# First layer norm of a gated attention and FFN block: rows scaled on ScalarE, `bn_aggr` for the moments, two buffers for the first values, output weights of the second head fetched three quads sooner

## The chip, the cores and the metric

One Trainium2 chip, one of its cores. The metric is the device time of one execution in microseconds (us), the median of several.

## What is computed

A block of a Flamingo model in fp32: 32 x 64 = 2048 rows `x` of 512, the same number of context rows, 32 query heads on 8 key/value heads of 128, causal within each batch entry, then a gated FFN of width 1792 whose weights are each multiplied by a product of rank 4.

```python
x = x + tanh(g_xattn[0]) * xattn(_layernorm(x), ctx, ctx, Wq, Wk, Wv, Wd)
x = x + tanh(g_ffn[0])  * ffn(_layernorm(x), ...)

def _layernorm(x, axis=-1, eps=1e-05):
    m = jnp.mean(x, axis=axis, keepdims=True)
    v = jnp.var(x, axis=axis, keepdims=True)
    return (x - m) / jnp.sqrt(v + eps)
```

## The kernel before, in words

Every fp32 product is made of three fp32r matmuls (`three_pass`, L503): each operand is split in a high part (a copy, on ScalarE) and a low part (the raw value less the high part, on VectorE or POOL). Each engine has its program written out by hand, with semaphores; the order in it is the order of the code, and an engine that waits holds all that stands behind.

The program has four parts. First the keys of half of the context (`keys`, to about 54 us). Then 44 **quads** q = 0 to 43 (to about 526 us), each a product of two by two blocks in Strassen's form with seven products of six matmuls each (`quad` and `product`, L558 to L610): quads 0 to 7 (NV = 8) make the values, 8 to 11 (NK = 4) the other keys, and from Q0 = 12 on the queries, 16 quads for each of two blocks of x. Then 64 attention units with the output product (L694), and the FFN.

A quad on TensorE runs the products 1, 6, 5, then (in some quads) the transposes of x, then 4, 2, 7, the one matmul of `effective` (L551, all quads but 7 and 8), and 3. ScalarE (L883) makes the high part of the next quad's weights (`left_hi`, L858), copies bank 0 to s1 (L894), splits two small factors `el`, `er` (`lr_hi`), copies bank 2 to s5 (L902), and writes a quarter of the result (L918). VectorE (L1167) makes t1 and t2 (L1173, L1185), the low halves of `el` and `er` (L1158), and three quarters of the result (L1196 to L1201); then `effective` (L1165). POOL (L1557) makes the low parts of the next weights (`left_lo`, L1470) and the sums for the quad after (`left_sums`, L1458 to L1463), in quads 0 to 5 the same for the context (`c_sums`, `c_combinations_lo`). SP issues all DMAs in one order (`quad_dmas`, L414): the last result's store, the store and load of `effective`, loads of context, weights, `el` and `er`, and x.

Between these the first layer norm is laid out in steps, for eight pairs of row tiles m = 0 to 7, four for each block of x:

```python
STATS = {q: m for m, q in enumerate((0, 3, 5, 7, 10, 13, 16, 19))}
APPLY, COLUMNS, X_SPLIT = ({q + n: m for q, m in STATS.items()} for n in range(1, 4))
```

In a STATS quad VectorE ends with `bn_stats` on `x_st` (L1122). In the APPLY quad it computes mean and variance + eps from them in seven small instructions (`ln_moments`, L1124 to L1135), POOL raises that to -1/2 (`ln_pow`, L1429), and VectorE ends the quad with (x - mean) * rstd in place (`apply1`, L1143). In the COLUMNS quad TensorE transposes the rows behind its third product (`columns`, L535), ScalarE copies them out (L840, L843), POOL sums them (`x_sums`). In the X_SPLIT quad they are split on ScalarE (L856) and at the end on VectorE (`x_lo`, L1152). The second layer norm uses the same `ln_moments` and `ln_pow` for n = 8 to 15, and POOL applies it (`apply2`).

The values leave from one buffer `v_st` (L357), so VectorE and ScalarE wait in quads 1 to 8 for the last store. The output weights of head k + 1 are fetched to one buffer `wd_raw` at every fourth unit (L474), the first of these in front of unit 2, and split on ScalarE (L928) and POOL (L1476) in the units of WD_STEP.

## Time and profile before

| | |
|---|---|
| median of 3 runs | 1510.31 us (1509.82 to 1510.69) |
| the profiled execution: time, span | 1507.59 us, 1505.6 us |
| mean granted TensorE clock | 0.998 |
| TensorE busy | 1475.6 us (98%) |
| VectorE, ScalarE, POOL busy | 1113.6 (74%), 638.5 (42%), 827.1 us (55%) |

The span goes from the first to the last instruction. A row of the timeline gives start and length in us, engine, line, operation, tile written and tiles read, shapes, the count of like instructions in a row, and in brackets how long the engine had been idle before it and what ended that. PE is TensorE, DVE VectorE, ACT ScalarE, POOL GpSimd, SPq the queue of SP. Matmuls overlap, so that one starts every 0.23 us and takes 0.39.

### The profile page before, as it was taken

The page shows a single profiled execution, that of the slowest core. Times are in us where ns is not written, and L with a number is a line of the kernel's source. Part 1 is how long each engine was busy: PE and PEld are TensorE (multiplying, and loading weights), DVE is VectorE, ACT ScalarE, POOL GpSimd, SP SyncE. Part 2 cuts the span into 40 slices and gives each one's busy share as a digit, 9 for nine tenths or more (in the row PEclk, how much of TensorE's full clock was granted, in tenths as well). Part 3 has the DMA queues.
Part 4 walks back from the last instruction along what each step waited for, and adds up shares of the span by engine and source line. Part 5 has one row for each costly group of instructions (what it writes and reads, how often), then busy time and mean ns, then how long its engine had stood idle before and what let it go on. Part 6 is the DMA issues. An engine that isn't in the chain of part 4 may idle for free.

```text
span 1505.6 us, 20729 instructions
## 1 busy us (share of the span) xinstructions
PE 1475.6 (98%) x7322; PEld 1176.3 (78%) x7322; DVE 1113.6 (74%) x1653; ACT 638.5 (42%) x1099; POOL 827.1 (55%) x716
## 2 busy tenths in 40 slices
PE   8999998999999999999999999999999999999998
PEld 8877777788888777777777777777788888888886
DVE  5387788876667767777777788778588897767676
ACT  5444444444444434344333444444344344434342
POOL 5598988887789311211211332234387877666663
PEclk9999999999999999999999999999999999999999
DMA  7466666767988553333333333342011111311112
GB/s 267 157 223 206 223 216 234 237 232 269 356 270 286 187 186 122 113 131 116 115 140 131 113 131 115 112 146 89 18 46 57 50 56 49 111 51 56 50 56 70
DMA packets 116070, 218.02 MB, mean 145 GB/s; under 512 B 9472, under 2 KB 47616, under 8 KB 113920
## 3 DMA queue, kind: packets, MB, share of 16 engines
q1 hardware_dynamic: 115968, 216.70, 42.7%
q8 instruction: 59, 0.97, 0.3%
q14 instruction: 43, 0.35, 0.1%
HBM read 151.13 MB, written 65.54 MB: 144 GB/s over the span
## 4 chain that ended last, share of the span: by engine, by line
PE 87%; DVE 8%; issue 2%; POOL 1%; DMA 1%; ACT 0%; SPq 0%; DVEq 0%; POOLq 0%; ACTq 0%
PE bank L507 63%; PE bank L659 4%; PE bank L621 4%; PE bank L772 3%; PE bank L774 3%; PE bank L773 3%; PE bank L630 2%; PE bank L644 2%; DVE x_st L1146 1%; DVE t L1185 1%; DVE el L1158 1%; DVE X L1322 1%; DVE xc L1152 1%; DVE er L1158 0%; PE bank L683 0%
## 5 line engine op out<-in xcount | busy, mean ns | idle before, releaser
L1476 POOL TENSOR_TENSOR wd_lo<-wd_raw,wd_hi 128x512 fp32r<-128x512 f32 x64 | 91.4, 1448 | 368.8 <-ACT wd_hi L928 368.8
L507 PE MATMUL bank<-xc,wa_hi 128*128 128x512 f32 x896 | 278.9, 392 | 1.1 <-DVE q_st L1201 0.8
L507 PE MATMUL bank<-wd_hi,o_hi 128*128 128x512 f32 x512 | 205.7, 402 | 0.0
L507 PE MATMUL bank<-wd_hi,o_lo 128*128 128x512 f32 x512 | 200.1, 391 | 0.0
L507 PE MATMUL bank<-wd_lo,o_hi 128*128 128x512 f32 x512 | 199.3, 389 | 0.0
L507 PEld LDWEIGHTS bank<-xc,wa_hi 128*128 128x128 f32 x896 | 167.9, 189 | 39.1 <-DVE q_st L1201 2.1
L507 PE MATMUL bank<-xc,wa_lo 128*128 128x512 f32 x448 | 175.0, 391 | 0.0
L1322 DVE SCALAR_TENSOR_TENSOR X<-bank,tg,X 128x512 f32<-128x512 f32 x224 | 156.4, 741 | 0.0
L507 PE MATMUL bank<-x_hi,wf_hi 128*128 128x512 f32 x392 | 153.0, 390 | 0.2 <-DVE d_lo L1310 0.2
L507 PE MATMUL bank<-x_hi,wf_lo 128*128 128x512 f32 x392 | 152.6, 389 | 0.0
L507 PE MATMUL bank<-x_lo,wf_hi 128*128 128x512 f32 x364 | 141.6, 389 | 0.0
L1217 DVE TENSOR_TENSOR prob<-bank,mask 128x512 f32<-128x512 f32 x64 | 44.3, 692 | 127.5 <-PE bank L630 125.8
L1470 POOL TENSOR_TENSOR wa_lo<-w_raw,wa_hi 128x512 fp32r<-128x512 f32 x72 | 83.2, 1176 | 55.1 <-ACT wa_hi L869 55.1
L507 PEld LDWEIGHTS bank<-wd_hi,o_lo 128*128 128x128 f32 x512 | 96.1, 188 | 20.8
L507 PEld LDWEIGHTS bank<-wd_lo,o_hi 128*128 128x128 f32 x512 | 96.4, 188 | 18.1
L507 PEld LDWEIGHTS bank<-wd_hi,o_hi 128*128 128x128 f32 x512 | 96.2, 188 | 17.9 <-DVE X L1255 0.3
L947 ACT ACTIVATE pt<-bank 128x512 f32<-128x512 f32 x64 | 38.2, 598 | 156.7 <-PE bank L644 156.7
L507 PEld LDWEIGHTS bank<-xc,wa_lo 128*128 128x128 f32 x448 | 84.4, 188 | 18.0
L1255 DVE SCALAR_TENSOR_TENSOR X<-bank,tg,X 128x512 f32<-128x512 f32 x128 | 90.6, 743 | 10.4 <-PE bank L507 10.4
L1517 POOL TENSOR_TENSOR wf_lo<-f_raw,wf_hi 128x512 fp32r<-128x512 f32 (+1 forms) x56 | 57.7, 1032 | 63.1 <-ACT wf_hi L988 62.8
L772 PE MATMUL bank<-dn_hi,d_hi 128*128 128x512 f32 x224 | 87.3, 390 | 0.9 <-DVE X L1322 0.9
L1014 ACT ACTIVATE d_hi<-bank 128x512 fp32r<-128x512 f32 x56 | 33.6, 600 | 128.9 <-DVE bank L1316 68.8
(179 smaller groups left out, 3504.3 us busy)
## 6 DMA issues: line engine op xcount, KB each, us to landing
q_scratch<-q_st SPq DMA_DIRECT2D x32, 1024.0 KB, 4.3
q_sb<-q_scratch SPq DMA_DIRECT2D x64, 512.0 KB, 3.3
w_raw<-in_wq SPq DMA_DIRECT2D x32, 512.0 KB, 4.3
wd_raw<-in_wd SPq DMA_DIRECT2D x16, 1024.0 KB, 4.9
f_raw<-ffn_eff_scratch SPq DMA_DIRECT2D x28, 512.0 KB, 3.6
er_raw<-in_sf_r SPq DMA_DIRECT2D x42, 256.0 KB, 3.6
e_raw<-in_wf SPq DMA_DIRECT2D x42, 256.0 KB, 5.2
ffn_eff_scratch<-e_eff SPq DMA_DIRECT2D x42, 256.0 KB, 5.0
```

The lines of the kernel that those rows point to most:

```text
L507: last = pe.matmul(to, a, b, start=(start and n == 0), stop=(stop and n == 3 * len(pairs) - 1), skip_group_check=onto)
L621: last = pe.matmul(bank[6][b * S:(b + 1) * S, t * 256:(t + 1) * 256], k_sb[u % 2][:, cb * S:(cb + 1) * S], q_sb[u % 2][:, :, cb, :, :].rea ...
L659: last = pe.matmul(bank[4 + b][:, t * 256:(t + 1) * 256], v_sb[u % 2][rows, t, :], pt[rows, t, :], start=True, stop=True)
L772: pe.matmul(to, d_hi[b][:, half, cols], dn_hi[n == NF - 1][:, :], start=True, stop=False)
L773: pe.matmul(to, d_hi[b][:, half, cols], dn_lo[n == NF - 1][:, :], start=False, stop=False)
L774: pe.matmul(to, d_lo[b][:, half, cols], dn_hi[n == NF - 1][:, :], start=False, stop=True).then_inc(p_yf, 1)
L1217: v.tensor_tensor(prob[:, :, :], bank[6][:, :].rearrange("p (n k) -> p n k", k=S), mask[:, :].rearrange("p (o k) -> p o k", o=1).broadcast ...
L1255: v.scalar_tensor_tensor(to, bank[t if u < NU - 1 else 4 + t][:, :], tg[:, 0:1], to, ALU.mult, ALU.add).then_inc(v_y, 1)
L1322: v.scalar_tensor_tensor(to, bank[4 + k % 4][:, :], tg[:, 1:2], to, ALU.mult, ALU.add).then_inc(v_yf, 1)
L1470: g.tensor_tensor(wa_lo[p][:, part, :, :].rearrange("p n k d -> p (n k d)"), raw, f32(wa_hi[p][:, part, :, :]).rearrange("p n k d -> p (n ...
L1476: g.tensor_tensor(wd_lo[h % 2][:, e, :], wd_raw[:, e, :], f32(wd_hi[h % 2][:, e, :]), ALU.subtract).then_inc(g_wd, 1)
L1517: g.tensor_tensor(wf_lo[:, cols, :, :].rearrange("p n k d -> p (n k d)"), raw, f32(wf_hi[:, cols, :, :]).rearrange("p n k d -> p (n k d)") ...
```

## The change

`bn_aggr` gives mean and variance from the six numbers of `bn_stats`, one instruction for each of two row tiles. VectorE then makes variance + eps and the negated mean, POOL the power and `shift` = -mean * rstd, and ScalarE computes x * rstd + shift in place, at the end of its APPLY quad. The last four row pairs are laid out four quads apart and not three. The values of quads 1 and 3 go to a second buffer, whose place is that of the first query weights, so that their load waits for the stores. `load_wd(1)` moves from the first unit to quad 41. Numbers of lines are those before.

```diff
-    STATS = {q: m for m, q in enumerate((0, 3, 5, 7, 10, 13, 16, 19))}
+    STATS = {q: m for m, q in enumerate((0, 3, 5, 7, 11, 15, 19, 23))}
...
+    V_BUFFER = (0, 1, 0, 1, 0, 0, 0, 0)
+    def v_stored(q):
+        return V_BUFFER[:q].count(V_BUFFER[q])
...
     def load_w(w):
             if w < 2:
                 sp.wait_ge(v_wvl, 7)
+                sp.wait_ge(d_vo[1], 16 * 2)
...
         for q in range(NQ):
             quad_dmas(q)
+            if q == NQ - 3:
+                load_wd(1)
...
-            if i % 4 == 0 and i // 4 + 1 < NWD:
+            if i % 4 == 0 and 0 < i and i // 4 + 1 < NWD:
                 load_wd(i // 4 + 1)
...
         def columns(m):
-                pe.wait_ge(v_xn, 2 * m + p + 1)
+                pe.wait_ge(a_xn, 2 * m + p + 1)
...
+        def apply1(m):
+            a.wait_ge(g_nm, m + 1)
+            for p in range(2):
+                a.activation(x_st[:, p, :], x_st[:, p, :], ACT.Identity, bias=shift[:, p:p + 1],
+                             scale=rstd[:, p:p + 1]).then_inc(a_xn, 1)
...
-            if 1 <= q <= NV:
-                a.wait_ge(d_vo, 16 * q)
+            if 2 <= q < NV:
+                a.wait_ge(d_vo[V_BUFFER[q]], 16 * v_stored(q))
...
             a.activation(result(q, 0, 0), split(q, bank[0][:, :]), ACT.Copy).then_inc(a_c11, 1)
+            if q in APPLY:
+                apply1(APPLY[q])
...
         def ln_moments(n):
             v.wait_ge(v_bn, 2 * n + 2)
-            v.tensor_tensor(mean[:, :], bn[:, :, 1], bn[:, :, 4], ALU.add).then_inc(v_ln, 1)
-            v.tensor_tensor(half_gap[:, :], bn[:, :, 1], bn[:, :, 4], ALU.subtract).then_inc(v_ln, 1)
-            v.tensor_tensor(veps[:, :], bn[:, :, 2], bn[:, :, 5], ALU.add).then_inc(v_ln, 1)
-            v.wait_ge(v_ln, 6 * n + 3)
-            v.tensor_scalar(mean[:, :], mean[:, :], 0.5, None, ALU.mult).then_inc(v_ln, 1)
-            v.scalar_tensor_tensor(half_gap[:, :], half_gap[:, :], 0.25, half_gap[:, :], ALU.mult,
-                                   ALU.mult).then_inc(v_ln, 1)
-            v.tensor_scalar(veps[:, :], veps[:, :], 1.0 / D, EPS, ALU.mult, ALU.add).then_inc(v_ln, 1)
-            v.wait_ge(v_ln, 6 * n + 6)
-            v.tensor_tensor(veps[:, :], veps[:, :], half_gap[:, :], ALU.add).then_inc(v_eps, 1)
+            if 1 <= n <= 8:
+                v.wait_ge(g_nm, n)
+            for p in range(2):
+                v.bn_aggr(moments[:, p, :], bn[:, p, :]).then_inc(v_ln, 1)
+            v.wait_ge(v_ln, 2 * n + 2)
+            v.tensor_scalar(veps[:, :], moments[:, :, 1], EPS, None, ALU.add).then_inc(v_eps, 1)
+            if n < 8:
+                v.tensor_scalar(neg_mean[:, :], moments[:, :, 0], -1.0, None, ALU.mult).then_inc(v_nm, 1)
...
-        def apply1(m):
-            v.wait_ge(g_pow, m + 1)
-            for p in range(2):
-                v.tensor_scalar(x_st[:, p, :], x_st[:, p, :], mean[:, p:p + 1], rstd[:, p:p + 1], ALU.subtract,
-                                ALU.mult).then_inc(v_xn, 1)
...
         def ln_pow(n):
             g.wait_ge(v_eps, n + 1)
+            if 1 <= n <= 8:
+                g.wait_ge(a_xn, 2 * n)
             g.tensor_tensor(rstd[:, :], veps[:, :], neg_half[:, :], ALU.pow).then_inc(g_pow, 1)
+            if n < 8:
+                g.wait_ge(g_pow, n + 1)
+                g.wait_ge(v_nm, n + 1)
+                g.tensor_tensor(shift[:, :], neg_mean[:, :], rstd[:, :], ALU.mult).then_inc(g_nm, 1)
```

How it moves instructions, at three places. VectorE from the moments of an apply quad to the next quad, in the kernel before (quad 11; mean, half_gap and veps are the small tiles):

```order
L1126 TENSOR_TENSOR mean<-bn 128x2
L1127 TENSOR_TENSOR half_gap<-bn 128x2
L1128 TENSOR_TENSOR veps<-bn 128x2
L1130 TENSOR_SCALAR mean<-mean 128x2
L1131 SCALAR_TENSOR_TENSOR half_gap<-half_gap 128x2
L1133 TENSOR_SCALAR veps<-veps 128x2
L1135 TENSOR_TENSOR veps<-veps,half_gap 128x2
L1185 TENSOR_TENSOR t_104<-bank,s_101 128x512
...
L1165 TENSOR_TENSOR e_eff<-bank,e_raw_110 128x512
L1146 TENSOR_SCALAR x_st<-x_st,mean,rstd 128x512 x2
L1173 TENSOR_TENSOR t_103<-bank,s_101 128x512
```

and of the change (quad 12):

```order
L1152 BN_AGGR moments<-bn 128x2 x2
L1154 TENSOR_SCALAR veps<-moments 128x2
L1156 TENSOR_SCALAR neg_mean<-moments 128x2
L1198 TENSOR_TENSOR t_106<-bank,s_103 128x512
...
L1178 TENSOR_TENSOR e_eff<-bank,e_raw_112 128x512
L1186 TENSOR_TENSOR t_105<-bank,s_103 128x512
```

Seven small instructions have become four, and the two on `x_st` are gone from between two quads.

ScalarE from the end of the apply quad (the quarter of the result) to the copy of bank 0 to s1, before:

```order
L918 ACTIVATE kq_98<-bank 128x4x128
L869 ACTIVATE wa_hi_93<-w_raw_87 128x512
L871 ACTIVATE wa_hi_93<-w_raw_87 128x256
L874 ACTIVATE wa_hi_93<-ws_91 128x1024
L894 ACTIVATE s_101<-bank 128x512
```

and of the change:

```order
L939 ACTIVATE q_st_101<-bank 128x4x2x64
L852 ACTIVATE x_st<-x_st,shift,rstd 128x512 x2
L888 ACTIVATE wa_hi_93<-w_raw_87 128x512
L890 ACTIVATE wa_hi_93<-w_raw_87 128x256
L893 ACTIVATE wa_hi_93<-ws_91 128x1024
L913 ACTIVATE s_103<-bank 128x512
```

The two activations on `x_st`, with their wait for `shift`, stand ahead of the next weights' high part.

SP at quad 41 of the change:

```order
L347 DMA el_raw_110<-in_sf_l 128x128
L348 DMA er_raw_108<-in_sf_r 128x512
L383 DMA wd_raw<-in_wd 128x2048
L377 DMA q_scratch<-q_st_102 128x4x512
L359 DMA ffn_eff_scratch<-e_eff 128x512
```

and, of the kernel before, where that load stood, behind the last quad:

```order
L367 DMA q_scratch<-q_st_100 128x4x512
L349 DMA ffn_eff_scratch<-e_eff 128x512
L373 DMA wd_raw<-in_wd 128x2048
L382 DMA q_sb_114<-q_scratch 128x1024
L384 DMA k_sb_122<-k_scratch 128x256
```

The load of the second head's output weights has gone ahead of the stores of the queries of quads 41, 42 and 43 and of four loads for the first units.

## Rows read from the trace of the kernel before

**Rows 1.** The page, section 1: busy us, share of the span, instructions.
```profile
PE 1475.6 (98%) x7322; PEld 1176.3 (78%) x7322; DVE 1113.6 (74%) x1653; ACT 638.5 (42%) x1099; POOL 827.1 (55%) x716
```
**Rows 2.** Waits of TensorE: us in total, times, longest.
```profile
PE bank L541 <- DVE x_st L1146: 11.4, 12, 2.0
...
PE bank L507 <- ACT v_st L918: 1.9, 1, 1.9
```
**Rows 3.** Timeline of TensorE: starts behind a wait, quads 5, 7, 9, 12.
```profile
110.81 0.50 PE L507 MATMUL bank<-wv_hi,cc 128*128 128x512 f32 x1 [0.31 <-DVE t L1185]
...
136.72 0.66 PE L541 MATMUL bank<-ident,x_st 128*128 128x128 f32 x4 [1.79 <-DVE x_st L1146]
...
159.31 0.66 PE L541 MATMUL bank<-ident,x_st 128*128 128x128 f32 x4 [1.98 <-DVE x_st L1146]
...
194.44 0.65 PE L541 MATMUL bank<-ident,x_st 128*128 128x128 f32 x4 [1.59 <-DVE x_st L1146]
```
**Rows 4.** Timeline of TensorE: transposes of quad 2; L551 of quads 11, 12, 13.
```profile
80.76 1.12 PE L541 MATMUL bank<-ident,x_st 128*128 128x128 f32 x8
81.64 0.47 PE L507 MATMUL bank<-wv_hi,cc 128*128 128x512 f32 x1
...
186.25 0.50 PE L551 MATMUL bank<-er,el 96*128 96x512 f32 x1
...
199.91 0.40 PE L551 MATMUL bank<-er,el 96*128 96x512 f32 x1
...
209.68 0.40 PE L551 MATMUL bank<-er,el 96*128 96x512 f32 x1
```
**Rows 5.** Timeline of VectorE: moments of quad 4; moments and rows of quad 11.
```profile
107.22 2.24 DVE L1126 TENSOR_TENSOR mean<-bn 128x2 f32<-128x2 f32 x1
...
186.22 0.58 DVE L1126 TENSOR_TENSOR mean<-bn 128x2 f32<-128x2 f32 x1
...
188.43 0.16 DVE L1135 TENSOR_TENSOR veps<-veps,half_gap 128x2 f32<-128x2 f32 x1
...
191.64 3.61 DVE L1146 TENSOR_SCALAR x_st<-x_st,mean,rstd 128x512 f32<-128x512 f32 x2
```
**Rows 6.** Timeline of POOL: the power in quad 8; around it in quad 11.
```profile
155.26 2.48 POOL L1431 TENSOR_TENSOR rstd<-veps,neg_half 128x2 f32<-128x2 f32 x1
...
187.56 0.74 POOL L1463 TENSOR_TENSOR ws<-w_raw,ws 128x256 f32<-128x256 f32 x1
188.67 0.70 POOL L1431 TENSOR_TENSOR rstd<-veps,neg_half 128x2 f32<-128x2 f32 x1 [0.37 <-DVE veps L1135]
189.34 2.44 POOL L1470 TENSOR_TENSOR wa_lo<-w_raw,wa_hi 128x512 fp32r<-128x512 f32 x2
```
**Rows 7.** Timeline of ScalarE at the start of quad 12.
```profile
188.24 0.63 ACT L869 ACTIVATE wa_hi<-w_raw 128x512 fp32r<-128x512 f32 x1 [2.83 <-PE bank L507]
...
190.03 0.58 ACT L894 ACTIVATE s<-bank 128x512 f32<-128x512 f32 x1
```
**Rows 8.** Windows: length, busy us (count) of PE, PEld, DVE, ACT, POOL; clock, DMA, GB/s.
```profile
160.40:163.80 3.40, 3.40 (x12) 2.72 (x11) 3.17 (x3) 0.80 (x2) 3.40 (x3) 0.52 0.25 83
228.70:232.10 3.40, 3.29 (x10) 2.82 (x11) 2.61 (x4) 1.13 (x2) 3.32 (x5) 0.51 0.91 299
```
**Rows 9.** The chain of waits, a DMA (start, us); timeline of TensorE in unit 3.
```profile
527.44 7.25 DMA wd_raw<-in_wd
...
536.40 1.14 PE L659 MATMUL bank<-pt,v_sb 64*128 64x256 f32 x8 [1.50 <-ACT pt L947]
```
**Rows 10.** DMA issues: count, KB each, median us from issue to landing.
```profile
v_scratch<-v_st SPq DMA_DIRECT2D x8, 1024.0 KB, 4.7
```
**Rows 11.** Groups of VectorE, 60 to 300 us: busy us, mean ns, idle before.
```profile
L1146 DVE TENSOR_SCALAR x_st<-x_st,mean,rstd 128x512 f32<-128x512 f32 x16 | 21.5, 1381 | 0.6 <-POOL rstd L1431 0.6
L1152 DVE TENSOR_TENSOR xc<-xb,xc 128x1792 fp32r<-128x1792 f32 x7 | 17.2, 2453 | 0.0
...
L1122 DVE BATCH_NORM_STATS2 bn<-x_st 128x6 f32<-128x512 f32 x16 | 10.2, 677 | 0.3 <-DMA x_st<-in_x 0.3
```

More of the change, by code:

```diff
@@ L75, in flamingo @@
     bn = at(1.34375, "bn", [P, 2, 6])
-    mean = at(1.40625, "mean", [P, 2])
-    half_gap = at(1.4375, "half_gap", [P, 2])
+    moments = at(1.40625, "moments", [P, 2, 2])
     veps = at(1.46875, "veps", [P, 2])
+    neg_mean = at(1.4375, "neg_mean", [P, 2])
     rstd = at(1.5, "rstd", [P, 2])
+    shift = at(1.625, "shift", [P, 2])
     row_max = at(1.53125, "row_max", [P, CB * G // 2])
@@ L112, in flamingo @@
     wa_lo = [at(170, "wa_lo0", [P, 7, 2, DK], F32R), at(154, "wa_lo1", [P, 7, 2, DK], F32R)]
-    v_st = at(177, "v_st", [P, HKV, CT, DK])
+    v_st = [at(177, "v_st0", [P, HKV, CT, DK]), at(185, "v_st1", [P, HKV, CT, DK])]
     kq = [at(177, "kq0", [P, 2, 4, C]), at(185, "kq1", [P, 2, 4, C])]
@@ L170, in flamingo @@
     d_c = [sem(f"d_cb{n}") for n in range(2)]
+    g_nm, a_xn, v_nm = sem("g_nm"), sem("a_xn"), sem("v_nm")
     d_ko = [sem(f"d_ko{n}") for n in range(4)]
-    d_vo = sem("d_vo")
+    d_vo = [sem(f"d_vo{n}") for n in range(2)]
     d_wq = [sem(f"d_wq{n}") for n in range(2)]
@@ L245, in result @@
         if q < NV:
-            return v_st[:, 4 * e:4 * e + 4, half, :]
+            return v_st[V_BUFFER[q]][:, 4 * e:4 * e + 4, half, :]
         if q < Q0:
@@ L357, in store_q @@
                 sp.dma_start(vd[:, q].rearrange("h p t d -> p h (t d)"),
-                             v_st[:, :, :, :].rearrange("p h t d -> p h (t d)")).then_inc(d_vo, 16)
+                             v_st[V_BUFFER[q]][:, :, :, :].rearrange("p h t d -> p h (t d)")).then_inc(d_vo[V_BUFFER[q]], 16)
                 return
@@ L454, in _ @@
                     sp.wait_ge(d_ko[n], 16 * NCH // 2)
-                sp.wait_ge(d_vo, 16 * NV)
+                sp.wait_ge(d_vo[0], 16 * V_BUFFER.count(0))
+                sp.wait_ge(d_vo[1], 16 * V_BUFFER.count(1))
                 for n in range(2):
@@ L911, in quad @@
             a.wait_ge(p_p[2], q + 1)
-            if 1 <= q <= NV:
-                a.wait_ge(d_vo, 16 * q)
+            if 2 <= q < NV:
+                a.wait_ge(d_vo[V_BUFFER[q]], 16 * v_stored(q))
+            if q == NV:
+                a.wait_ge(d_vo[0], 16 * V_BUFFER.count(0))
             if 2 <= w < NK + 2:
@@ L1125, in ln_moments @@
             v.wait_ge(v_bn, 2 * n + 2)
-            v.tensor_tensor(mean[:, :], bn[:, :, 1], bn[:, :, 4], ALU.add).then_inc(v_ln, 1)
-            v.tensor_tensor(half_gap[:, :], bn[:, :, 1], bn[:, :, 4], ALU.subtract).then_inc(v_ln, 1)
-            v.tensor_tensor(veps[:, :], bn[:, :, 2], bn[:, :, 5], ALU.add).then_inc(v_ln, 1)
-            v.wait_ge(v_ln, 6 * n + 3)
-            v.tensor_scalar(mean[:, :], mean[:, :], 0.5, None, ALU.mult).then_inc(v_ln, 1)
-            v.scalar_tensor_tensor(half_gap[:, :], half_gap[:, :], 0.25, half_gap[:, :], ALU.mult,
-                                   ALU.mult).then_inc(v_ln, 1)
-            v.tensor_scalar(veps[:, :], veps[:, :], 1.0 / D, EPS, ALU.mult, ALU.add).then_inc(v_ln, 1)
-            v.wait_ge(v_ln, 6 * n + 6)
-            v.tensor_tensor(veps[:, :], veps[:, :], half_gap[:, :], ALU.add).then_inc(v_eps, 1)
+            if 1 <= n <= 8:
[6 more added lines that the diff above has]
+                v.tensor_scalar(neg_mean[:, :], moments[:, :, 0], -1.0, None, ALU.mult).then_inc(v_nm, 1)
         def stats1(m):
             v.wait_ge(d_x, 16 * (m + 1))
-            if m:
-                v.wait_ge(v_xn, 2 * m)
             ln_bn(lambda p: x_st[:, p, :])
-        def apply1(m):
-            v.wait_ge(g_pow, m + 1)
-            for p in range(2):
-                v.tensor_scalar(x_st[:, p, :], x_st[:, p, :], mean[:, p:p + 1], rstd[:, p:p + 1], ALU.subtract,
-                                ALU.mult).then_inc(v_xn, 1)
         def x_lo(m):
@@ L1189, in quad @@
             v.wait_ge(a_s5, q + 1)
-            if 1 <= q <= NV:
-                v.wait_ge(d_vo, 16 * q)
+            if 2 <= q < NV:
+                v.wait_ge(d_vo[V_BUFFER[q]], 16 * v_stored(q))
+            if q == NV:
+                v.wait_ge(d_vo[0], 16 * V_BUFFER.count(0))
             if 2 <= w < NK + 2:
@@ L1207, in quad @@
                 stats1(STATS[q])
-            if q in APPLY:
-                apply1(APPLY[q])
         rows = [P, CB * G // 2, S]
@@ L1483, in apply2 @@
             for p in range(2):
-                g.tensor_scalar(xn2[:, p, :], X[:, 2 * m + p, :], mean[:, p:p + 1], rstd[:, p:p + 1], ALU.subtract,
+                g.tensor_scalar(xn2[:, p, :], X[:, 2 * m + p, :], moments[:, p, 0:1], rstd[:, p:p + 1], ALU.subtract,
                                 ALU.mult).then_inc(g_xn, 1)
```

## The prediction

> **What bounds the kernel.** I read the page first: TensorE is busy for 1475.6 us, 98% of the span [rows 1], so only the 30 us in which it stands still, and what stretches its matmuls, can be won. Next, whom it waits for: 11.4 us in 12 waits go to the normalised rows `x_st` that VectorE writes at L1146, and 1.9 us are one wait for ScalarE's L918 in quad 1 [rows 2]; the start waits for its first loads. Then where these waits lie. All 12 are in the transposes of `columns`, as a pair each (the second 0.21 us), in quads 7, 9, 12, 15, 18 and 21. The first wait of the pair in 7, in 9 and in 12 can be seen [rows 3]; the pairs of 15, 18 and 21 repeat that of 12. The transposes of quads 2 and 5 find their rows ready.
>
> An idle gap understates its price, so I take whole quads, from one matmul of `effective` (L551) to the next. A plain quad takes 209.68 - 199.91 = 9.77 us, quad 12 takes 199.91 - 186.25 = 13.66 [rows 4]. Eight transposes with no wait push the next matmul back by 81.64 - 80.76 = 0.88 us [rows 4], and I add 0.15 for the refill behind them. So a stalled quad loses 13.66 - 9.77 - 1.03 = 2.86 us: 1.8 is the pair, the rest a short wait for L1201 of the quad before and the restarts. A product is 6 of the 43 matmuls of a plain quad, 1.36 us.
>
> Why the rows are late: in quad 11 VectorE is at the moments from 186.22 to 188.59 [rows 5], so POOL's power runs only from 188.67 to 189.37 [rows 6], and L1146 comes last in VectorE's quad, from 191.64 to 195.25, its two halves taking 3.61 us beside POOL's L1470 [rows 5, 6]. TensorE wanted the first half at 194.44 - 1.59 = 192.85 [rows 3].
>
> Last, the clock. From 160.4 to 163.8 the granted clock is 0.52, the 1.2 GHz level [rows 8], right behind the 1.98 us wait of quad 9 [rows 3]. A second stretch of the same length, from 228.7, follows the wait of quad 15 [rows 8]. 3.4 us at half rate cost 1.7 us.
>
> **The change part by part.** *Rows on ScalarE.* VectorE loses its 16 L1146, 21.5 us [rows 11], and each set of seven small instructions becomes four; none of this is on the path by itself. ScalarE gains 16 activations of 128x512 and POOL 8 products of 128x2. An activation of that size takes 0.60 to 0.63 us [rows 7], so a pair is 1.2. The product I price as POOL's power of the same shape, 0.70 [rows 6].
>
> I place them in quad 12 (apply) and 13 (transposes) of the changed kernel, with T the start of 13. The old apply quad 11 ends, and quad 12 begins, at about 188.2 (L551 at 186.25, one restart and a product behind it), and there POOL's sums end at 188.30, T + 0.1 [rows 6]. The power waited for the moments; it no longer does, as the split `x_lo` (L1152, 2.45 us [rows 11]) now lies a quad ahead of the stats. So power and product end at T + 1.5, ScalarE's pair at T + 2.7. TensorE wants it after three products, at T + 4.1. The four waits of quads 13, 17, 21 and 25 go: 4 x 2.86 = **11.4**.
>
> What stands behind the new wait on ScalarE: `left_hi` (from 188.24, 1.8 us) and the copy to s1 at 190.03 [rows 7]. They now end at T + 4.5 and T + 5.1; s1 was done at T + 2.4. TensorE needs s1 after four products and the transposes, at T + 6.5: 1.4 us to spare, and about as much for the matmul of `effective`, which wants VectorE's two low halves (L1158) behind ScalarE's next two copies. `left_hi` feeds POOL's L1470, which starts 2.7 us later, takes under 5 and is due at the next quad, T + 10.8: hidden. If this cover were gone, each quad would pay what is missing, first at s1. Cost 0.
>
> *Quads 2, 5, 7 and 9.* In quad 7 POOL has its sums done early: 1.79 + 0.21 of idle and 0.3 of restarts go, **2.3**. Quads 2 and 5 have no such wait, and the ScalarE pair in front of their s1 fits the same slack: **0**. Quad 9 is different. Its power starts at 155.26, behind sums that waited for a weight load, and takes 2.48 because VectorE's L1152 has the way [rows 6]. It ends at 157.74, the product at 158.4, ScalarE's first half at 159.1: just where L1146 let the transposes go before (159.31) [rows 3]. Behind it `left_hi`, s1 and the halves for `effective` would each be 0.5 to 1 late. Bounds: 4.1 won (2.4 of the wait, 1.7 of clock) if POOL gets in ahead of L1152; 1.5 lost if the follow-on waits come and the clock falls as before. I take **0**, since the time of the first half (159.1) and the old one (159.31) are the nearest rows.
>
> *Clock.* The fall of quad 15 has lost the wait ahead of it: **1.7**. That of quad 9 is in its bounds.
>
> *Moments.* In quad 4 the first of the seven is held 2.24 us by POOL's running instruction [rows 5], and TensorE stands 0.31 us, early in quad 5, for the late L1185 [rows 3], and again for L1201. The trace has no joining instruction. Between the small rows (0.16 [rows 5]) and `bn_stats` (0.68 [rows 11]) I take 0.2 each, as it reads 6 numbers. The epsilon step behind it may be held all the same. Nothing or 1.1 us (two gaps and their restarts): **0.4**, nearer to the held row.
>
> The Trainium skill says that GpSimd shares its SBUF interfaces with VectorE and contends with instructions of two SBUF inputs or in a two-port mode (GPSIMD Engine Reference, 8. Key points). By that rule the joining instruction goes free but the epsilon step could be held as L1126 was, and the 0.4 would be 0; the trace agrees with the rule on L1126, and has no case of so small a tensor_scalar that asks first.
>
> The Trainium skill also prices an activation's per-partition operand, about 93 ns for each `[128,1]` scale or bias (ScalarE: Activation LUTs, What ACT_TABLE_LOAD costs). No activation of the kernel before that stands in these quads has one. By it the pair would be an estimated 1.6 us, quad 9 would lose 0.4 more and the sum would be 0.4 less; elsewhere it stays under the cover.
>
> *Two buffers for the values.* The store of `v_st` lands in 4.7 us [rows 10], and no wait that TensorE has [rows 2] leads back to it, so nothing is gained. SP now waits in quad 4 for the store that it has just issued, 4.7 us, ahead of a weight load that is wanted in quad 7. **0.**
>
> *Output weights.* wd_raw is issued at 527.44 and lands 7.25 us later; behind it on ScalarE stand L928 and the copy to `pt` for which TensorE waits 1.50 us [rows 9]. Issued in quad 41, three quads sooner, it is long there. It passes the stores of two quads on SP and holds them back by about its own landing; each is wanted two quads on. **1.5.**
>
> *Spacing.* As many quads as before follow an `x_lo`, and none has the stats on top. **0.**
>
> Sum: 11.4 + 2.3 + 1.7 + 0.4 + 1.5 = **17.3 us**. Against the profiled execution's own 1507.59 us that is 1490.3. The timed runs have their median at 1510.31, 2.7 above it; the difference taken from there gives **1493.0 us**. Within 0.2% (3 us) a measurement of this kernel can't tell it from no change.
>
> **The rivals.**
> *ScalarE passes half of it on (14%).* The transposes find their rows but s1 or `effective` is late, as in my quad 9. For: ScalarE now waits on POOL, which has hardly a gap in these quads. Against: 1.4 us of slack. It decides once the product ends after T + 2.9. At 1.2 us in each of six quads 7 us are lost again: 1500.
> *POOL's answer comes too late everywhere (4%), slower.* If power and product are held in every apply quad as at 155.26 (2.48 each) and start 1 us later, the rows come at T + 7.3 and no wait goes; s1 and `effective` add 1.2 in each of eight quads. It decides once the pair ends after T + 6. With 8 x 1.2 = 9.6 lost against the 1.5 of the weights: 1518. Against it: in quad 11 the power took 0.70.
> *The rows are late for another reason (4%).* The change would then not do what it says: the wait moves from L1146 to L852 with the same end, and only the weights' 1.5 is won: 1509.
> *Quad 9 clears too (14%).* 4.1 us more: 1489.
> *Forecast (64%): 1493.*
>
> The range reaches below the last and over the first: **1487.5 to 1501**; one or two more falls of the clock (1.7 each) are in it. It leaves out the second and third rival and some of each tail. Faster 0.92, within 0.2% 0.04, slower 0.04.
>
> **What would show it.** In the profile after: no wait at the transposes of quads 7, 13, 17, 21 and 25, and a quad of 10.8 us there; a wait of about 2 us left in quad 9, now for ScalarE's line; rstd and shift ending within 1.5 us of the next quad's start; no wait at 536; a span near 1488. It is wrong if the copy to s1 or the low halves of er appear among TensorE's releasers in those quads, if the pair takes much over 1.6 us, or if the clock falls in new places.

## Result, and the profile after

The changed kernel takes 1491.1 us in the median (1489.67 to 1491.44, 4 runs), beside 1510.07 (1506.81 to 1510.69, 4 runs) for the kernel before: a ratio of 0.9877, 95% interval 0.986 to 0.9894. The forecast was 1493.0 and its range held the time. Of the reasons behind it the largest does not hold: the 11.4 us of the late quads that I gave to ScalarE's rows, the new moments bring alone.

The page of the changed kernel, section 1 [rows 1]:

```profile
PE 1469.6 (99%) x7322; PEld 1175.0 (79%) x7322; DVE 1082.7 (73%) x1581; ACT 647.8 (43%) x1115; POOL 828.7 (56%) x724
```

Whom TensorE waits for in it (us in total, times, longest) [rows 2]:

```profile
PE bank L520 <- DVE wk_lo L1345: 6.5, 2, 5.7
PE bank L564 <- DVE er L1171: 2.6, 3, 1.1
PE bank L520 <- ACT v_st L939: 1.9, 1, 1.9
PE bank L554 <- ACT x_st L852: 1.8, 1, 1.8
```

The 11.4 us for `x_st` have become 1.8, in quad 9 alone, and a new releaser stands above them: the low half of `er`, in three waits. No line for `pt` is left. The first wait is the start of the program. TensorE's timeline in quads 9, 11, 12 and 13 of the changed kernel (L564 is the old L551, L554 the old L541) [rows 3, 4]:

```profile
156.98 1.36 PE L554 MATMUL bank<-ident,x_st 128*128 128x128 f32 x8 [1.77 <-ACT x_st L852]
...
159.94 0.73 PE L520 MATMUL bank<-cc,wa_hi 128*128 128x512 f32 x2 [0.21 <-ACT s L913]
...
163.92 0.50 PE L564 MATMUL bank<-er,el 96*128 96x512 f32 x1 [0.97 <-DVE er L1171]
...
184.82 0.50 PE L564 MATMUL bank<-er,el 96*128 96x512 f32 x1 [1.07 <-DVE er L1171]
...
194.71 0.40 PE L564 MATMUL bank<-er,el 96*128 96x512 f32 x1
...
200.40 1.03 PE L554 MATMUL bank<-ident,x_st 128*128 128x128 f32 x8
```

The transposes of quad 13 find their rows. Quad 9 still waits 1.77 us for its rows, then a little for s1, then 0.97 us for `er`.

For an account I cut the span at the matmul of `effective`, as the prediction did; quads 7 and 8 have none, so 7 to 9 are one piece. It is in us, from the trace of each kernel:

| piece | before | changed |
|---|---|---|
| start to quad 0 | 62.57 | 63.11 |
| quads 1 to 6 | 66.51 | 66.31 |
| quads 7 to 9 | 37.34 | 34.50 |
| quads 10 to 28 | 204.45 | 192.42 |
| quads 29 to 43 | 152.23 | 152.23 |
| the rest | 982.49 | 981.05 |
| span | 1505.59 | 1489.63 |

The two traces are 16.0 us apart, the medians 19.0, where 17.3 was forecast. 12.0 of the 16.0 us come from quads 10 to 28, 2.8 from 7 to 9, 1.4 from the weights. In quads 1 to 6 the 1.1 us won in quads 4 and 5 is nearly used up by quad 1, which is 1.6 longer and whose follower is 0.6 shorter: the clock fell there (below). The 0.5 us before quad 0 is scatter of the start, which lies between 62.5 and 63.6 us in these kernels.

Now the new operations in quad 12 of the changed kernel: VectorE's small instructions, POOL's power and product, ScalarE's pair of rows [rows 5, 6, 7]:

```profile
193.19 0.25 DVE L1152 BATCH_NORM_AGGREGATE moments<-bn 128x2 f32<-128x6 f32 x2
193.47 0.31 DVE L1154 TENSOR_SCALAR veps<-moments 128x2 f32<-128x2 f32 x1
193.70 0.15 DVE L1156 TENSOR_SCALAR neg_mean<-moments 128x2 f32<-128x2 f32 x1
```
```profile
195.23 0.70 POOL L1446 TENSOR_TENSOR rstd<-veps,neg_half 128x2 f32<-128x2 f32 x1
196.01 0.36 POOL L1450 TENSOR_TENSOR shift<-neg_mean,rstd 128x2 f32<-128x2 f32 x1
```
```profile
196.41 1.52 ACT L852 ACTIVATE x_st<-x_st,shift,rstd 128x512 f32<-128x512 f32 x2 [2.27 <-POOL shift L1450]
```

Two joining instructions take 0.25 us together. POOL is free by 195.27, ahead of the start of quad 13 (about 196.6), so the pair is done 1.3 us after it. I had it at 2.7.

### The profile page after: what moved, and what is told of

It reads as the page before. It is cut to its first block, busy times and chain, and to the rows that moved or that the text cites. A ratio compares the mean times of both kernels' runs of the same rounds, so it can differ in the third digit from the quotient of the medians.

```text
span 1489.6 us, 20699 instructions
## 1 busy us (share of the span) xinstructions
PE 1469.6 (99%) x7322; PEld 1175.0 (79%) x7322; DVE 1082.7 (73%) x1581; ACT 647.8 (43%) x1115; POOL 828.7 (56%) x724
## 4 chain that ended last, share of the span: by engine, by line
PE 90%; DVE 5%; issue 2%; POOL 1%; DMA 1%; ACT 1%; SPq 0%; DVEq 0%; ACTq 0%; POOLq 0%
PE bank L520 65%; PE bank L672 5%; PE bank L634 4%; PE bank L785 3%; PE bank L786 3%; PE bank L787 3%; PE bank L643 3%; PE bank L657 2%; DVE el L1171 1%; PE bank L564 1%; DVE X L1335 1%; DMA c_raw<-in_ctx_t 1%; DVE er L1171 1%; PE bank L696 0%; DVE xc L1165 0%
## 5 line engine op out<-in xcount | busy, mean ns | idle before, releaser
L1536 POOL TENSOR_TENSOR wf_lo<-f_raw,wf_hi 128x512 fp32r<-128x512 f32 (+1 forms) x56 | 57.7, 1033 | 63.6 <-ACT wf_hi L1011 63.3
L1489 POOL TENSOR_TENSOR wa_lo<-ws,wa_hi 128x1024 fp32r<-128x1024 f32 x36 | 90.4, 2511 | 0.0
```

The costliest lines, as they stand in the source:

```text
L1489: g.tensor_tensor(wa_lo[p][:, part, :, :].rearrange("p n k d -> p (n k d)"), raw, f32(wa_hi[p][:, part, :, :]).rearrange("p n k d -> p (n ...
L1536: g.tensor_tensor(wf_lo[:, cols, :, :].rearrange("p n k d -> p (n k d)"), raw, f32(wf_hi[:, cols, :, :]).rearrange("p n k d -> p (n k d)") ...
```

## The experiments

Twelve kernels, each beside the kernel before on its chip; ratios are against those runs, whose medians lay between 1508.5 and 1509.7 us. Three stretches of each trace stand in the table at the end of this section.

### One part undone

**rows_on_vector.** The rows go back to VectorE, at the end of its APPLY quad; all else is the change.

```diff
-            if q in APPLY:
-                apply1(APPLY[q])          # ScalarE
+            if q in APPLY:
+                apply1(APPLY[q])          # VectorE, tensor_scalar: subtract, mult
```

> The change with the x rows scaled on VectorE again at the end of the apply quad (joining instruction, spacing of four, two value buffers and early output weights kept; no product on POOL). If ScalarE's taking over the rows is what won the time, the pair of waits at the transposes comes back in the quads 7, 9, 13, 17, 21 and 25. It should be shorter than the 1.8 us of before, since power and veps now come earlier, but L1146 alone stands behind effective until about 3.5 us into the quad and takes 1.5 to 3.6: 1 to 2 us of idle in each, 8 to 14 us more than the change, 1499 to 1505. Rival, the shorter moments and the wider spacing did it: then these waits stay away and the time stays within 2 us of the change, 1491.

Measured: 1494.08 us, ratio 0.9905 (0.989 to 0.992). TensorE's waits in it:

```profile
PE bank L554 <- DVE x_st L1153: 4.2, 4, 2.0
```

All four are in quads 7 and 9. The time is 3.0 us above the change, well short of the 8 to 14 that the theory asked for, and the rival's account of the late quads holds. The column quads 13, 17, 21 and 25 take 10.7 us, as in the change: with rows on VectorE they wait for nothing. So ScalarE's rows don't explain the late quads; they pay in quads 7 to 9 alone, where this kernel takes 38.80 us to the change's 34.50 (two falls of the clock are in the 38.80).

**old_spacing.** The statistics every third quad again.

```diff
-    STATS = {q: m for m, q in enumerate((0, 3, 5, 7, 11, 15, 19, 23))}
+    STATS = {q: m for m, q in enumerate((0, 3, 5, 7, 10, 13, 16, 19))}
```

> The change with the row pairs 4 to 7 laid out three quads apart as before (10, 13, 16, 19). The forecast priced the spacing at 0: the split of VectorE and the stats then stand together in one quad again, so effective in the apply quads is late by 0.3 us or a little more, the same count of quads as now; the small moments no longer delay L1185. Within 1.5 us of the change, 1490 to 1493. Rival, the spacing carries a good part of the gain: the power is late again, ScalarE hands the delay on and each of the four quads pays 1 to 3 us: 1495 to 1503.

Measured: 1497.34 us, ratio 0.9929 (0.9914 to 0.9943): 6 us of the change's gain are gone. No column quad waits for rows; `er` is late in 11 quads:

```profile
PE bank L564 <- DVE er L1171: 7.2, 11, 1.1
```

The product is late here and `er` behind it, as in my first rival. ScalarE and VectorE of this kernel in quad 12, whose first product starts about 186.5:

```profile
188.07 1.52 ACT L852 ACTIVATE x_st<-x_st,shift,rstd 128x512 f32<-128x512 f32 x2 [5.35 <-POOL shift L1450]
...
191.28 0.58 ACT L913 ACTIVATE s<-bank 128x512 f32<-128x512 f32 x1
```
```profile
191.99 0.69 DVE L1186 TENSOR_TENSOR t<-bank,s 128x512 f32<-128x512 f32 x1 [3.68 <-ACT s L913]
192.71 1.98 DVE L1171 TENSOR_TENSOR el<-el_raw,el 32x128 fp32r<-32x128 f32 x1
194.71 1.11 DVE L1171 TENSOR_TENSOR er<-er_raw,er 32x512 fp32r<-32x512 f32 x1
```

Here the pair pushes s1 back on ScalarE. TensorE doesn't need s1 yet, but VectorE's t1 does, and VectorE stood idle 3.68 us for it; `el` and `er` stand behind t1, and `el` takes 1.98 beside POOL. They end at 195.82, and TensorE's matmul of them starts at 195.88. In the change the pair starts 0.2 us ahead of the column quad (196.41 to about 196.6), here 1.6 us behind its start; so there `er` is ready. The spacing sets this. At the old one `x_lo` (the low half of the transposed rows, on VectorE) runs in the quad ahead of the power, and POOL's first two low parts beside it (128x512 and 128x256, one row of the timeline) take 3.77 us, to 2.00 in quad 12 of the change (from 187.51); the power then starts at 187.07, 0.6 us behind the column quad's start.

But s1 is the smaller half of the loss. The column quads take 11.3 us, 0.5 more than joining_only's 10.8 (below). Quads 11, 14, 17, 20 and 23, right behind an `x_lo`, take 11.0 to its 10.06, and they are 4.8 of the 7.4 us that the two kernels differ by in quads 10 to 28. The delay comes to them through POOL: its low parts wait for `left_hi`, which stands behind the pair on ScalarE, and it is still 1 us late in the quad after. POOL and VectorE in quad 13 of joining_only and then of this kernel (its matmul of `effective` is at 205.97 there, at 205.76 here):

```profile
208.55 3.78 POOL L1477 TENSOR_TENSOR wa_lo<-w_raw,wa_hi 128x512 fp32r<-128x512 f32 x2 [0.36 <-ACT wa_hi L878]
209.30 2.44 DVE L1155 TENSOR_TENSOR xc<-xb,xc 128x1792 fp32r<-128x1792 f32 x1
```
```profile
209.31 3.77 POOL L1489 TENSOR_TENSOR wa_lo<-w_raw,wa_hi 128x512 fp32r<-128x512 f32 x2
209.65 2.84 DVE L1165 TENSOR_TENSOR xc<-xb,xc 128x1792 fp32r<-128x1792 f32 x1
```

In both `x_lo` ends 3.2 us behind POOL's start, though it begins 0.75 us behind it in the one and 0.34 in the other. In this kernel the first of POOL's two low parts gives way to the second at 210.56, and `x_lo` ends 1.9 us after that: it looks as if `x_lo` were held until the first is done, which these rows suggest and no run isolates. t1, `el` and `er` stand behind `x_lo`.

**weights_late.** The second head's output weights at the first unit again.

```diff
-            if q == NQ - 3:
-                load_wd(1)
...
-            if i % 4 == 0 and 0 < i and i // 4 + 1 < NWD:
+            if i % 4 == 0 and i // 4 + 1 < NWD:
```

> The change with the load of the second head's output weights back at the first unit. One wait of 1.5 us of TensorE for ScalarE's pt copy, at the third weighted_values, and nothing else: 1.5 us more than the change, 1492.6, quads unchanged. Rival, the early load also delayed or hastened other transfers: another difference in the last quads.

Measured: 1491.76 us, ratio 0.9891 (0.9876 to 0.9905). The wait for `pt` is back with its 1.5 us, and the rest behind quad 43 takes 982.46 us, to the change's 981.05: the weights are worth 1.4.

**seven_moments.** The change with the seven small instructions; rows on ScalarE.

```diff
-            for p in range(2):
-                v.bn_aggr(moments[:, p, :], bn[:, p, :]).then_inc(v_ln, 1)
...
+            v.tensor_tensor(mean[:, :], bn[:, :, 1], bn[:, :, 4], ALU.add).then_inc(v_ln, 1)
...
+            v.tensor_tensor(veps[:, :], veps[:, :], half_gap[:, :], ALU.add).then_inc(v_eps, 1)
```

> The change with the seven small instructions in place of bn_aggr; rows still on ScalarE. Theory (the moments are off the path in all quads but 4, 5 and 8, 9): 0.4 to 1 us more than the change, ratio 0.988 to 0.9885. Rival (the joining instruction is what lets POOL's power and product come in time): waits for ScalarE's x_st at L554 come back in the late quads, or s1 and er become late by some tenths in each: 3 us or more, ratio 0.990 or over.

Measured: 1494.26 us, ratio 0.9901 (0.9887 to 0.9916), 3 to 4 us more. The rival's size came, by its second way: the column quads wait for nothing (10.7 us each), but `er` is late in seven quads, and the quads right behind an `x_lo` (15, 19, 23, 27) have grown from 10.07 to 10.7 or 10.8:

```profile
PE bank L566 <- DVE er L1179: 5.8, 7, 1.1
```

It is the path through POOL again. The longer moments hold ScalarE's pair of quad 12 back to 196.99, from 196.41 in the change, and POOL's low parts in quad 14 start 3.3 us behind the matmul of `effective`, not 2.6; so `x_lo`, which stands ahead of t1, `el` and `er`, ends 0.7 us later. Quad 14 of this kernel:

```profile
218.40 3.77 POOL L1497 TENSOR_TENSOR wa_lo<-w_raw,wa_hi 128x512 fp32r<-128x512 f32 x2
218.74 2.83 DVE L1173 TENSOR_TENSOR xc<-xb,xc 128x1792 fp32r<-128x1792 f32 x1
```

The change has both forms: POOL late in quad 10, behind the late rows of quad 9, with `er` late in 11, and POOL early in quad 14, with `er` in time in 15:

```profile
177.35 3.78 POOL L1489 TENSOR_TENSOR wa_lo<-w_raw,wa_hi 128x512 fp32r<-128x512 f32 x2
177.70 2.83 DVE L1165 TENSOR_TENSOR xc<-xb,xc 128x1792 fp32r<-128x1792 f32 x1
...
217.74 3.78 POOL L1489 TENSOR_TENSOR wa_lo<-w_raw,wa_hi 128x512 fp32r<-128x512 f32 x2
218.83 2.09 DVE L1165 TENSOR_TENSOR xc<-xb,xc 128x1792 fp32r<-128x1792 f32 x1
```

**one_value_buffer.** The change with one buffer for the values.

```diff
-    V_BUFFER = (0, 1, 0, 1, 0, 0, 0, 0)
+    V_BUFFER = (0, 0, 0, 0, 0, 0, 0, 0)
```

> The change with one buffer for the first values, as before. Theory (nothing TensorE waits for leads back to the store of v_st): the change's own time, ratio 0.9872 to 0.9882. Rival (the store's landing held ScalarE's and VectorE's first copies in quads 1 to 3, and the buffer took that away): waits for the copies to v_st come back in quads 1 to 3, 0.5 to 2 us more, ratio 0.988 to 0.989.

Measured: 1490.44 us, ratio 0.9876 (0.9859 to 0.9892): the change's own. The second buffer is worth nothing.

### One part alone

**joining_only.** The kernel before with `bn_aggr` and the epsilon step in place of the seven; rows on VectorE, statistics every third quad, one buffer, late weights.

```diff
-            v.tensor_tensor(mean[:, :], bn[:, :, 1], bn[:, :, 4], ALU.add).then_inc(v_ln, 1)
...
+            for p in range(2):
+                v.bn_aggr(moments[:, p, :], bn[:, p, :]).then_inc(v_ln, 1)
+            v.wait_ge(v_ln, 2 * n + 2)
+            v.tensor_scalar(veps[:, :], moments[:, :, 1], EPS, None, ALU.add).then_inc(v_eps, 1)
```

> The kernel before with one part of the change: bn_aggr in place of the seven small instructions' first six and the epsilon step on its result; rows on VectorE, statistics every third quad. Theory (the moments stand on the path of the late rows, and the joining takes 1.35 us out of it as between spacing_only and rows_on_vector, 12.04 to 10.69 us in a column quad): 13.66 falls to about 12.3 in the four late quads, and quads 7 to 9 gain some tenths: 5.5 to 6.5 us less than before, ratio 0.996. Rival (with the old spacing x_lo stands between the apply quad's start and the moments and POOL is busy when they end, so the shorter chain only waits for POOL): under 3 us, ratio over 0.998.

Measured: 1493.94 us, ratio 0.9902 (0.9887 to 0.9916). That is 15.3 us (14.0 between the traces) from four small instructions fewer per pair of row tiles, more than twice what I expected even at that stage. The four late column quads fall from 13.66 to 10.8 us. VectorE and TensorE of this kernel, quads 11 and 12, to be held against [rows 5] with 0.84 us added (this kernel is so much earlier at L551):

```profile
185.39 0.25 DVE L1138 BATCH_NORM_AGGREGATE moments<-bn 128x2 f32<-128x6 f32 x2
185.67 0.30 DVE L1140 TENSOR_SCALAR veps<-moments 128x2 f32<-128x2 f32 x1
185.89 0.68 DVE L1188 TENSOR_TENSOR t<-bank,s 128x512 f32<-128x512 f32 x1
...
189.00 1.97 DVE L1149 TENSOR_SCALAR x_st<-x_st,moments,rstd 128x512 f32<-128x512 f32 x2
```
```profile
191.23 1.03 PE L550 MATMUL bank<-ident,x_st 128*128 128x128 f32 x8
```

Two gains add up. The moments end 1.8 us sooner (185.97 + 0.84 against 188.59), and with them everything behind them in VectorE's queue; the pair starts at 189.84 on the old scale, not at 191.64. And it takes 1.97 us, not 3.61, and now runs beside POOL's two smaller low parts, no longer beside the one of 128x1024, here at 190.66:

```profile
188.52 2.17 POOL L1477 TENSOR_TENSOR wa_lo<-w_raw,wa_hi 128x512 fp32r<-128x512 f32 x2
190.66 2.57 POOL L1477 TENSOR_TENSOR wa_lo<-ws,wa_hi 128x1024 fp32r<-128x1024 f32 x1
```

In the kernel before, that one ran from 191.74 and the pair from 191.64. That the company makes the length is read from such rows; no run changes it alone. So the pair ends 3.4 us sooner, at 191.81 on the old scale, and TensorE wanted the first half at 192.85.

**spacing_only.** The kernel before with the new quads for the statistics, and nothing else.

> The kernel before with the statistics' quads alone changed, to 0, 3, 5, 7, 11, 15, 19, 23; rows on VectorE, seven small instructions for the moments, one value buffer and late weights as before. Theory (the spacing makes the late column quads' rows punctual, since x_lo of the block before no longer stands in the apply quad): the four pairs of waits of the late quads go without ScalarE, those of quads 7 and 9 stay with the clock fall behind quad 9. 4 x 2.86 = 11.4 and one clock fall of 1.7 less than before: about 1496, ratio 0.991 to 0.992. Rival (the seven instructions, or VectorE's own two passes, keep the rows late even so): waits for L1146 stay at quads 13, 17, 21 and 25, and the time is 1503 or more, ratio over 0.996.

Measured: 1500.9 us, ratio 0.9947 (0.9932 to 0.9962); between theory and rival. The waits at quads 13, 17, 21 and 25 stay, shorter; these quads take 12.0 us. With `x_lo` out of the quad before, the moments start sooner, but they are as long as before, and the pair still meets POOL's large low part and takes 3.46.

```profile
PE bank L541 <- DVE x_st L1146: 8.7, 8, 2.0
```

**rows_on_scalar_only.** The kernel before with the rows on ScalarE, and POOL's product; the seven small instructions are kept.

> The kernel before with one part of the change: the rows go to ScalarE, with POOL's product; statistics every third quad, seven small instructions, one value buffer and late weights as before. This is the step that my prediction priced at 11.4 us in the late quads and 2.3 in quad 7. If that pricing holds, 13 to 15 us less than before, ratio 0.990 to 0.991. Theory now (with x_lo in the apply quad and the long moments, what the rows gain goes to er and s1, as in old_spacing, where each late group of three quads still took 32.2 us against 33.5): about 1.3 us in each of four groups and 3 us in quads 7 to 9, 8 us less than before or fewer, ratio 0.9945 to 0.997.

Measured: 1501.27 us, ratio 0.9948 (0.9934 to 0.9963): 7.9 us, where my prediction had given this step 13.7 and 1.7 of clock. The late groups of three quads take 32.6 us (quads 12 to 14: 11.64, 9.89 and 11.03), to 33.5 before and 30.6 in joining_only: the rows are in time, `er` is not. Quads 11 and 14, behind an `x_lo`, have the 11.0 us of old_spacing.

```profile
PE bank L562 <- DVE er L1175: 4.8, 6, 1.1
PE bank L552 <- ACT x_st L850: 2.1, 1, 2.1
```

### Quads 7 to 9, and what is left

**power_first_q8.** The change, with POOL's power and product ahead of the sums in quad 8, where POOL stands idle for the weights.

```diff
+            if q == 8:
+                ln_pow(APPLY[q])
             if 0 <= w + 2 < NW:
                 left_sums(w + 2)
-            if q in APPLY:
+            if q in APPLY and q != 8:
                 ln_pow(APPLY[q])
```

> The change with POOL's power and product ahead of the left sums in quad 8 alone. In the profile of the change POOL stands idle there for 2.4 us waiting for a weight load while veps is ready at 147.6, and the power runs at 155.1 only. Theory (POOL's order makes quad 9 late, and its follow-on the 1.07 us of quad 11): the 1.77 us at the transposes of quad 9, the 0.21 and 0.97 behind it and about 0.9 of quad 11 go: 4 to 4.5 us less than the change, 1486.5 to 1487.2. Rival (the rows wait for ScalarE's or VectorE's own work): quad 9 keeps its wait, within 1 us of the change.

Measured: 1487.28 us, ratio 0.9863 (0.9846 to 0.988). POOL in quad 8 of the change, and then of this kernel:

```profile
150.08 0.74 POOL L1477 TENSOR_TENSOR ws<-w_raw 128x256 f32<-128x256 f32 x1 [2.43 <-DMA w_raw<-in_w]
...
152.75 2.40 POOL L1482 TENSOR_TENSOR ws<-w_raw,ws 128x256 f32<-128x256 f32 x1
155.11 0.70 POOL L1446 TENSOR_TENSOR rstd<-veps,neg_half 128x2 f32<-128x2 f32 x1
155.88 0.20 POOL L1450 TENSOR_TENSOR shift<-neg_mean,rstd 128x2 f32<-128x2 f32 x1
```
```profile
146.18 0.70 POOL L1446 TENSOR_TENSOR rstd<-veps,neg_half 128x2 f32<-128x2 f32 x1
146.96 0.20 POOL L1450 TENSOR_TENSOR shift<-neg_mean,rstd 128x2 f32<-128x2 f32 x1
148.53 0.74 POOL L1477 TENSOR_TENSOR ws<-w_raw 128x256 f32<-128x256 f32 x1 [1.38 <-DMA w_raw<-in_w]
```

The power moves into idle time, over 7 us sooner in its quad (it ran at 155.11, and this kernel is 1.5 us ahead by quad 6); the wait of quad 9 is gone and quads 7 to 9 take 31.36 us, 3.1 less. ScalarE, too, is free by then, and its pair runs at 147.45. Whether the move would pay with rows on VectorE, where the pair stands behind `x_lo`, no run shows. The 0.9 us that I expected in quad 11 did not come: quads 10 and 11 take 20.90 us in both kernels. The median is 3.8 us below the change's; the traces are 4.7 apart, and 1.5 of that lies in quads 1 to 6, where this trace has no fall of the clock.

**power_first_x_lo_late.** The same, and six of the eight `x_lo` behind the moments of the next quad.

```diff
+            if X_SPLIT.get(q - 1) in LATE:        # LATE = (0, 3, 4, 5, 6, 7)
+                x_lo(X_SPLIT[q - 1])
```

> power_first_q8 with one more part: x_lo of six of the eight blocks stands behind the moments of the quad after, no longer ahead of el and er. Theory (where the stats stand every fourth quad, x_lo of 2.0 to 2.8 us in the quad before the matmuls of effective is what makes er late, 1.07 us in quad 11 and 0.97 us behind quad 9): the waits of L564 for L1171 fall from 1.4 us to under 0.5, and the time is 1.5 to 2 us under power_first_q8, about 1485.5, ratio 0.985. Rival (er is late for ScalarE's copies, or x_lo is as costly in its new place because the columns' low parts are then late): the time of power_first_q8, ratio 0.9863, or more.

Measured: 1487.09 us, ratio 0.9856 (0.9841 to 0.9871): no difference. The mechanism was right where I had read it: the matmul of `effective` waits 0.4 us for `er` in all, and quad 11 takes 9.77, not 10.64 as in power_first_q8. But quad 12 takes 10.33 us, behind a first wait for `xc`, and quad 28 10.31; quads 10 to 28 are only 0.7 us shorter together (191.70 to 192.43), and the clock fell in quad 1 of its trace.

**scalar_for_three_blocks.** power_first_q8 with ScalarE's rows for blocks 1 to 3 only.

> power_first_q8 with ScalarE's rows for blocks 1 to 3 alone (column quads 5, 7 and 9); the other five blocks' rows on VectorE as in rows_on_vector. Theory (with the new spacing and the joining instruction VectorE is in time in the late quads, 10.69 us with either engine, so ScalarE's part pays in quads 7 and 9 alone): the time of power_first_q8 within 0.7 us, ratio 0.9855 to 0.9868. Rival (ScalarE's pair is worth something in the late quads too, which rows_on_vector's fewer waits for er hid): 2 us or more above power_first_q8, ratio 0.988.

Measured: 1487.67 us, ratio 0.9858 (0.9841 to 0.9874): the same as power_first_q8. In the late quads, at the new spacing, either engine does.

**first_four_on_scalar.** power_first_q8 with ScalarE's rows for blocks 0 to 3, VectorE's for 4 to 7, and the old spacing.

> power_first_q8 with ScalarE's rows for blocks 0 to 3 alone, VectorE's for 4 to 7, and the statistics back at every third quad. Theory (the joining instruction alone makes the late rows punctual, and both the new spacing and ScalarE's rows there only add column quads' company: quads 10 to 28 take 191.4 us in joining_only and 192.4 in power_first_q8): 1 us less than power_first_q8, 1486.3, ratio 0.985 to 0.986; column quads of about 10.8 us at 12, 15, 18 and 21, no wait at L554 there. Rival (the earlier quads 7 to 9 of ScalarE's form leave VectorE or POOL behind when the old spacing asks for the statistics of quad 10): waits for er or x_st in quads 10 to 12, ratio 0.987 or more.

Measured: 1487.21 us, ratio 0.9861 (0.9844 to 0.9877): the same again, not the 1 us less that I expected. The column quads are 10.8 us and wait for nothing, but quad 11 takes 10.99 us (`er` is late), not joining_only's 10.06, which uses the microsecond up. These four kernels beat both the kernel before and the change, whose median lies 3.4 to 4 us above theirs and whose span 3.0 to 5.2 us. That they beat the change rests on their times, at most 1488.38 us to its 1489.67 at least, and on the 3 us of quads 7 to 9; their ratios, 0.9856 to 0.9863, have intervals that overlap its own. They are not told apart; I would keep power_first_q8, the smallest edit.

### The parts side by side

Us from the traces. A star marks one fall of the clock in the stretch.

| kernel | moments, rows, spacing | quads 7 to 9 | quads 10 to 28 |
|---|---|---|---|
| before | seven, VectorE, old | 37.34 * | 204.45 * |
| spacing_only | seven, VectorE, new | 37.31 * | 196.75 |
| rows_on_scalar_only | seven, ScalarE, old | 34.85 * | 200.06 |
| seven_moments | seven, ScalarE, new | 34.36 | 195.12 |
| joining_only | joined, VectorE, old | 37.31 * | 191.36 |
| rows_on_vector | joined, VectorE, new | 38.80 ** | 191.30 |
| old_spacing | joined, ScalarE, old | 34.38 | 198.78 |
| the change | joined, ScalarE, new | 34.50 | 192.42 |

Quads 10 to 28 show it: the joining instruction alone takes 13.1 us out, a fall of the clock among them, and neither other part adds to that. With it in place, ScalarE's rows cost 7.4 us at the old spacing (191.36 to 198.78), and the new spacing gives 6.4 of that back. Quads 7 to 9 depend on the rows' engine alone, 2.5 to 3 us. Singly the three parts won 15.3, 8.8 and 7.9 us, 32 in sum; together, with the weights, 19.0. They overlap, since each works on the lateness of the same four pairs of rows.

One relation runs through quads 10 to 28 of all traces but that of power_first_x_lo_late, which moves `x_lo`. Each of their 65 `x_lo` ends 3.17 to 3.20 us behind the start of POOL's first low part, whether it takes 2.08 or 2.85 us itself. Where POOL starts 2.6 us behind the matmul of `effective`, the next quad takes 10.04 to 10.07 us; where it starts 3.5 us behind, 11.0.

## Why the prediction was right, and where not

**What bounds the kernel**: right. The gain came from idle time in front of the transposes, with its restarts, and from the falls of the clock behind it; a late column quad fell from 13.66 to 10.7 us, where I had 10.8.

**The step that failed is the attribution, in two terms.** "Moments" was put at 0.4 us, read from what TensorE waits for in quads 4 and 5. Alone they win 13.1 us in quads 10 to 28, the 11.4 and 1.7 that I had written under "Rows on ScalarE" and "Clock", and 0.7 in quads 4 and 5. I had all the rows: moments of 2.37 us in VectorE's queue, the power waiting for them, the pair at its end of 3.61 us beside POOL's L1470, the first half 1.59 us late. From "VectorE loses ... none of this is on the path by itself" I went on without pricing the other way to make the pair early, which is to take 1.8 us out ahead of it. Nor did I ask what the pair would then stand beside: half of the 3.4 us that it gained is that, by the rows. The sum came out by luck in this respect, because the same 11.4 us of waiting can be taken away only once.

**Rows on ScalarE**: "What stands behind ... cost 0" is wrong for the old spacing and nearly right for the new. I checked that TensorE gets s1 in time and gave `effective` "about as much", but passed over two things. VectorE's t1 waits for s1 and has `el` and `er` behind it. And "hidden", for `left_hi` feeding POOL, was asked of TensorE alone: POOL's delay lengthens the next `x_lo`. In old_spacing TensorE waits 7.2 us in all for `er`. Its product ends 1.6 us behind the start of the column quad, where I had placed it (T + 1.5) at no cost, and the kernel takes 7.4 us more in quads 10 to 28 than joining_only. My first rival (14%) had this loss and its size, but not the condition: it asked for a product after T + 2.9, and 1.6 was late enough. The change was saved because its power started 1.4 us before the quad, not 0.1 behind the start; I had not foreseen that, and it is luck.

**Spacing**: "0" holds with the joining instruction and rows on VectorE (191.36 and 191.30 us), and only there. In the change as it stands it is worth 6.4 us.

**Quads 7 to 9**: 2.3 for quad 7 and 0 for quad 9 were forecast, 2.84 measured. Power and product in quad 8 took 1.0 us, not 3.1 as the held row suggested, from nearly the old place (155.11), so the transposes start 2.3 us sooner than behind L1146 (156.98 to 159.31). But TensorE brought 2.4 us along from quad 7, as forecast, and quads 8 and 9 won only 0.4: what they gained by the missing fall of the clock they mostly lost at s1 and `er` (0.21 and 0.97 us). "Bounds" was the right form.

**Quad 11**: missed. `er` is late there by 1.07 us behind the `x_lo` of quad 10, which ends late because POOL is late; it takes 11.01 us, to 10.06 before.

**Clock**: both falls of the kernel before are gone, of which I had counted one; what the one in quad 9 was worth is within the 2.84. One is new, in quad 1: 1.6 us there, 1.0 with the 0.6 that quad 2 then doesn't wait.

**Weights** 1.4, with 1.5 forecast; **buffers** 0, as forecast.

**Prices**: the pair 1.52 us, I had 1.2 (from rows that say 0.58 and 0.63 for one, not 0.60 to 0.63). Each activation with two per-partition operands takes 0.81 us. The Trainium skill gives about 93 ns for each such operand (ScalarE: Activation LUTs, What ACT_TABLE_LOAD costs), and the trace agrees. The product takes 0.20 to 0.59 us and 0.33 in the mean, not the power's 0.70; a joining instruction 0.17, with 0.2 forecast.

## To carry to other kernels

Where an operation comes too late, write down its whole chain and price every member that the change touches, the smallest too: a few instructions of 128x2 ahead of it in the queue can be worth as much as moving it to another engine. Where a change does several things, ask of each what is left of the wait if it were the only one; if two of them remove it, the sum holds but says nothing about which to keep. When work is put on an idle engine, follow what stands behind it through a second engine, not only to TensorE, and ask what a later third engine will run beside.
